# A two-layer transformer kernel on one core: prologue laid out anew, rows of maxima issued by ScalarE, last chunk worked by pairs of token tiles

## The reference

```
x0 = x0 + g_msa * mha(mod(ln(x0)))          # and x1 alike
x  = x + g_mca * cross(x0 <-> x1);  x = x + g_mlp * mlp(mod(ln(x)))
x  = ln(x + mha(x, mask)) ; x = ln(x + mha(x, ctx)) ; x = ln(x + mlp(x))
```

## Time and profile before

| what | value |
|---|---|
| median of 3 runs | 2251.17 us (2240.67 to 2251.61) |
| the profiled execution's own time | 2249.42 us |
| its span, first to last instruction | 2247.5 us |
| TensorE busy | 2020.5 us, 90% |
| VectorE, ScalarE, GpSimd busy | 1547.9, 1287.5, 552.3 us |
| maxima products L1415 | 2048, 526.3 us |
| score products L1394 and value products L1441 | 4224 each, 612.9 and 584.1 us |
| exponentials L1608 | 2112, 1100.8 us |

### The profile page before, as it was taken

The page is one execution under the profiler, slowest core; times in us unless marked ns, Lnnn a source line. Parts: engine busy times, 40 slices in busy tenths (PEclk is TensorE's granted clock), DMA queues, the critical chain, the costliest instruction groups (busy, mean ns, idle before and its releaser), DMA issues. The chain is left out here.

```text
span 2247.5 us, 33863 instructions
## 1 busy us (share of the span) xinstructions
PE 2020.5 (90%) x12890; PEld 794.0 (35%) x12890; DVE 1547.9 (69%) x2835; ACT 1287.5 (57%) x2406; POOL 552.3 (25%) x526
## 2 busy tenths in 40 slices
PE   4699899897979999998999888999999999999975
PEld 2423233332323343533533532332253335335324
DVE  4577689796967759476377457896757985895703
ACT  1035577565745677765675643678235874784650
POOL 0027586642132301032121332210103011101100
PEclk9769999998989999999999996999699999999987
DMA  6615243322052302035034431200120020000000
GB/s 150 135 57 127 74 133 84 102 58 48 17 136 61 76 5 54 20 69 121 8 75 96 76 77 55 58 20 21 34 47 28 4 49 4 13 16 4 13 16 11
DMA packets 97304, 126.65 MB, mean 56 GB/s; under 512 B 25293, under 2 KB 81982, under 8 KB 92014
## 3 DMA queue, kind: packets, MB, share of 16 engines
q1 hardware_dynamic: 97134, 124.42, 23.3%
HBM read 89.95 MB, written 24.74 MB: 51 GB/s over the span
## 5 line engine op out<-in xcount | busy, mean ns | idle before, releaser
L1608 ACT ACTIVATE PT<-ps 128x512 f32<-128x512 f32 (+1 forms) x2112 | 1100.8, 602 | 697.0 <-PE ps L1394 691.1
L1677 DVE TENSOR_REDUCE mx<-ps 128x1 f32<-128x512 f32 x2048 | 1283.3, 682 | 270.9 <-PE ps L1415 267.1
L1415 PE MATMUL ps<-KS,QS 49*128 49x512 bf16 x2048 | 526.3, 403 | 132.0 <-DVE mx L1677 78.7
L1394 PE MATMUL ps<-QS,KS 51*128 51x512 bf16 (+3 forms) x4224 | 612.9, 389 | 0.3
L1441 PE MATMUL ps<-PT,Vt 128*32 128x512 f32 (+1 forms) x4224 | 584.1, 626 | 0.0
L1415 PEld LDWEIGHTS ps<-KS,QS 49*128 49x128 bf16 x2048 | 146.2, 95 | 726.6 <-DVE mx L1677 479.8
L1394 PEld LDWEIGHTS ps<-QS,KS 51*128 51x128 bf16 (+3 forms) x4224 | 209.9, 97 | 255.3 <-ACT PT L1608 86.0
L1908 POOL CAST nm<-nm 128x16 bf16<-128x16 f32 x64 | 12.6, 197 | 524.4 <-DVE nm L1690 524.2
L1441 PEld LDWEIGHTS ps<-PT,Vt 128*32 128x32 f32 (+1 forms) x4224 | 84.3, 109 | 147.2 <-issue 144.6
L1536 PE MATMUL ps<-XT,big 128*128 128x256 f32 x512 | 125.7, 396 | 2.4 <-ACT big L1650 1.4
L1547 PE MATMUL ps<-big 128*128 128x256 f32 x512 | 114.7, 382 | 2.1 <-DVE big L1810 2.1
(11 more groups left out here) (104 smaller groups left out, 1076.8 us busy)
## 6 DMA issues: line engine op xcount, KB each, us to landing
scr<-S SPq DMA_DIRECT2D x28, 768.0 KB, 3.6
big<-in_mask_1x1xSxS_ik SPq DMA_DIRECT2D x16, 1024.0 KB, 4.8
QS<-scr SPq DMA_DIRECT2D x32, 384.0 KB, 8.5
KS<-scr SPq DMA_DIRECT2D x24, 384.0 KB, 8.4
QS<-scr SPq DMA_DIRECT2D x32, 256.0 KB, 4.9
ON<-Oe SPq DMA_DIRECT2D x256, 32.0 KB
OD<-scr_r SPq DMA_DIRECT2D x32, 256.0 KB
KS<-scr SPq DMA_DIRECT2D x24, 256.0 KB, 4.5
```

What stands on the lines that cost most here:

```text
L1394: z = eng.matmul(ps[0:w, it.bank[j], :], KS[lo:hi, part, pr, col:col + w], QS[lo:hi, part, u.qs, pr, :], start=part == 0, stop=part == 1 a ...
L1415: return eng.matmul(mbank(it)[:, 0:w], QS[lo:lo + MR, 0, u.qs, pr, 128 * it.tq:128 * it.tq + 128], KS[lo:lo + MR, 0, pr, it.lo:it.hi], sta ...
L1608: eng.activation(PT[0:w, it.pt * 4 + 2 * it.pp + j, :], ps[0:w, it.bank[j], :], ACT.Exp, scale=0.25).then_inc(S["exp_done"], 1)
L1677: eng.tensor_reduce(out=mx[:, u.b, c, it.i:it.i + 1], in_=mbank(it)[:, 0:it.hi - it.lo], axis=AX.X, op=ALU.max).then_inc(S["max_done"], 1)
```

## The change

Prologue: the memset of the V tile goes from the plan to VectorE's head. The head of SyncE loads only the bias columns it needs at once (`colb0_in`), then the constant rows, `bb` and `vb`; the other seven columns, chunks 2 and 3 of `x` and the two later parts of `ada_w` come as one item `late_load` after the transfers of K and Q. `mod_g` of modulation 0 is put behind Q of chunk 0; the first Q gets buffers of its own (`Qf[2]` = OD, `S3s[2]` in `big`) and a semaphore `scr_q`. Rows are read back in two parts: part 0 of K0, Q0, K1 first, then part 1 of all. Q of chunk 1 is now made by the ordinary way (GpSimd splits it). Modulations 1 and 2 and the gate bias leave `beside` and become the first five entries of `side`.

Maxima: the two transfers `QS<-mr` become an item of their own, `m_move`, one step later, on ScalarE.

Denominators: `dd<-Oe` is issued ahead of the four `ON<-Oe`, with a semaphore `d_out` for which VectorE's reciprocal waits. ScalarE's copy to `Oe` waits for `d_out` too.

Last chunk: `last_l1` in place of the general chain.

```diff
@@ do_qk, split
+                    quick_rows.append((lambda: to_dram(it), lambda part: to_rows(it, (part,))))
@@ fin_b
+                of, it = it, Item("m_move")
+                it.u, it.last, it.mr = u, of.last, of.mr
                 it.qs_free = mark.get(("qs_free", u.qs))
                 dma(it, "m_in", 2)
+                fins.append([FIN - 1, lambda: plan.append(it)])
@@ norm, nc_
+                for lo, hi in ((0, 256), (256, CH)) if at["tail"] else ((0, CH),):
+                    it = item("norm_c")
@@
+        def last_l1(c):
+            at["tail"] = True
+            flush_norms()
+            do_out(c, None, (1, 1), (0,))
+            do_stats(c, 1e-5, 1, 0, 2)
+            do_out(c, None, (1, 1), (2,))
+            do_lnscale(c, 1, 1, 0, 2)
+            do_stats(c, 1e-5, 1, 2, 2)
+            do_xt("x", c, cols=256)
+            do_hid(c, True, 24, 0, 0)
+            do_lnscale(c, 1, 1, 2, 2)
+            for hp in range(1, 4):
+                do_hid(c, True, 24, 0, hp)
+            do_xt("x", c, cols=256, t0=2)
+            do_mout(c, 0, 2, None, (0, 0))
+            do_hid(c, True, 24, 1, 0)
+            do_stats(c, 1e-5, 0, 0, 2)
+            for hp in range(1, 4):
+                do_hid(c, True, 24, 1, hp)
+            do_lnscale(c, 2, 0, 0, 2)
+            store(c, 0, 2)
+            for t in (2, 3):
+                do_mout(c, t, 1, None, (0, 0))
+            for t in (2, 3):
+                do_stats(c, 1e-5, 0, t, 1)
+                do_lnscale(c, 2, 0, t, 1)
+                store(c, t, 1)
+            at["tail"] = False
@@ prologue
         do_stats(0, 1e-6)
-        modulation(0)
         do_xnorm(0)
-        item("ones_v")
+        modulation("mod_t", 0)
         do_stats(1, 1e-6)
         do_xt("mod", 0, 0)
         do_xnorm(1)
-        drain(k_steps(0, 512, "k_in0", [], 0, 0, True))
-        drain(q_steps(0, 0, 0, 0, True))
+        drain(k_steps(0, 512, "k_in0", [], 0, 0, 1))
+        drain(q_steps(0, 0, 0, 0, 2))
+        (k0_out, k0_rows), (q0_out, q0_rows) = quick_rows
+        k0_out()
+        q0_out()
+        k0_rows(0)
+        q0_rows(0)
         do_xt("mod", 1, 0, 512, 1)
-        drain(k_steps(512, 512, "k_in1", [], 0, 1, True))
+        modulation("mod_g", 0)
+        drain(k_steps(512, 512, "k_in1", [], 0, 1, 1))
+        k1_out, k1_rows = quick_rows[2]
+        k1_out()
+        k1_rows(0)
+        for rows in (k0_rows, q0_rows, k1_rows):
+            rows(1)
+        item("late_load")
@@ beside
-        beside = [second_v, second_q, lambda: modulation(1), lambda: modulation(2),
-                  lambda: gate_bias(0, I["L0_xattn_attn_proj_b"])]
+        beside = [second_q, second_v, first_v]
@@
+        side.extend([lambda kind=kind, g=g: modulation(kind, g) for g in (1, 2) for kind in ("mod_t", "mod_g")])
+        side.append(lambda: gate_bias(0, I["L0_xattn_attn_proj_b"]))
-... early=[lambda: None, first_v])
+... early=[lambda: None, lambda: None])
@@ SyncE, evict_out
+                    load(eng, dd[32 * hg:32 * hg + 32, ob, :], Oe[16:128:32, 0, :], "d_out")
                     for j in range(4):
                         load(eng, ON[lo:lo + 16, hg // 2, :], Oe[32 * j:32 * j + 16, 0, :], "o_out")
-                    load(eng, dd[32 * hg:32 * hg + 32, ob, :], Oe[16:128:32, 0, :], "o_out")
@@ ScalarE
+                elif it.kind == "m_move":
+                    q.wait_ge(S["mr_done"], it.mr)
+                    q.wait_ge(S["m_in"], it.was)
+                    q.wait_ge(S["m_ready"], it.last)
+                    if it.qs_free is not None:
+                        q.wait_ge(S[it.qs_free[0]], it.qs_free[1])
+                    for t in range(2):
+                        load(eng, QS[49 + t:50 + t + 64:64, 0, u.qs, 2 * u.hg:2 * u.hg + 2, :], mr[16 * t:16 * t + 16, u.b, :], "m_in")
```

More of the change, by code:

```diff
@@ L254, in half @@
                 it.w = n["wq_in"] if q else n["wkv_in"]
-                it.qf_free = mark.get("qf_free") if quick else mark["xn_free"]
+                it.qf_free = mark.get(("qf_free", quick)) if quick else mark["xn_free"]
                 take_m(it)
@@ L272, in split @@
                     flush_ends()
-                later.extend([[SPLIT[0], flush_ends], [SPLIT[1], lambda: to_dram(it)]])
-                if quick:
-                    flush_later()
+                    quick_rows.append((lambda: to_dram(it), lambda part: to_rows(it, (part,))))
+                else:
+                    later.extend([[SPLIT[0], flush_ends], [SPLIT[1], lambda: to_dram(it)]])
             def split_end(of):
@@ L283, in to_dram @@
                 it = item("split_out")
-                it.cols, it.low = cols, of.low
+                it.cols, it.low, it.quick = cols, of.low, quick
                 of.k = it.k = 4 + slot if q else n["scr_use"] % 4
@@ L294, in to_dram, with to_rows @@
                     held_rows[slot] = lambda: to_rows(of)
-            def to_rows(of):
+            def to_rows(of, parts=(0, 1)):
                 it = item("split_in")
                 it.q, it.cols, it.lo, it.slot, it.k, it.out = q, cols, lo, slot, of.k, of.out
+                it.scr_sem, it.parts = of.scr_sem, parts
                 it.over = [mark[k] for k in [("qs_free", slot)] if k in mark] if q else over
                 it.lo_was, it.lo_sem = n[name.replace("in", "lo")], name.replace("in", "lo")
[L301 to L307, removed]
+                if 1 in parts:
+                    mark["scr_free", it.k] = (it.lo_sem, up(it.lo_sem, 32))
+                    if not q:
+                        mark["klo", name] = mark["scr_free", it.k]
+                if 0 in parts:
+                    dma(it, name, 4)
+                    if q:
+                        taken[slot] = True
+                    else:
+                        mark["k", name] = (name, it.landed)
             def second():
@@ L521, in do_out @@
             x_done, xn_free = n[f"x_done{c}"], mark["xn_free"]
-            for lo in (0, 2):
+            for lo in tiles:
                 it = item("out")
-                it.ot, it.w = n["ot_done"], n["wp_in"]
+                it.ot, it.w = n["ot_done"] - (1 if at["tail"] and lo == 0 else 0), n["wp_in"]
                 take_m(it)
@@ L900, in mlp0, with store @@
             return ln_mod(c, 2) + mlp_chain(c, False, 16, 2, (0, c // 2))
-        def mlp1(c):
[L903 to L920, removed]
+        def store(c, lo=0, nt=4):
+            it = item("store")
+            it.c, it.lo, it.nt = c, lo, nt
+            x_state(it, c)
+            dma(it, "y_out", 1)
@@ L921, in modulation @@
+        def modulation(kind, g):
+            it = item(kind)
+            it.g = g
+            it.ada = 16
+            take_m(it)
+            if kind == "mod_t":
+                it.t, it.done = up("mod_t"), up("mod_done")
+                give_m(it, ("mod_t", it.t))
+                return
+            give_m(it, ("mod_g", up("mod_g")))
             if g == 0:
@@ L1105, in fast @@
             bg_until(999)
-            at["tail"] = False
         def load_mask(c):
@@ L1266, in sp_part @@
                     for part, lo, t, k in ((0, 0, 0 if it.q else 2, 1), (0, 16, 0 if it.q else 1, 2), (1, 0, 0, 3)):
+                        if part not in it.parts:
+                            continue
                         if part == 1:
@@ L1380, in sp_part @@
                     q.wait_ge(S["y_out"], it.was)
-                    load(eng, chunk(out, it.c), x[:, 4 * it.c:4 * it.c + 4, :], "y_out")
+                    lo = 4 * it.c + it.lo
+                    load(eng, chunk(out, it.c)[:, it.lo:it.lo + it.nt, :], x[:, lo:lo + it.nt, :], "y_out")
         def pe_part(eng, q, items):
```

198 lines of the change are left out of this document (116 added, 82 removed), and 2 rows, old and new, of the table S.

## The result

The changed kernel takes 2235.37 us (median of 4 runs, 2233.78 to 2237.55), the kernel before 2251.39 in the same series (4 runs). The ratio is 0.993, 95% interval [0.9911, 0.995]: 16 us faster, where 33 were forecast. The profiled execution took 2233.78 us, span 2231.9.

| stretch | before | after | difference | forecast |
|---|---|---|---|---|
| start to first scores | 118.6 | 82.7 | -36.0 | -38.6 |
| first scores to the end of unit 0 | 48.6 | 63.2 | +14.7 | +11 |
| end of unit 0 to last copy of `Oe` (the middle) | 2003.6 | 2018.9 | +15.3 | +6 |
| last copy of `Oe` to the end | 76.7 | 67.1 | -9.6 | -10.8 |

What follows compares the result with a forecast made beforehand. TensorE was taken to bound the 2053 us middle, between a 118.6 us prologue and a 76 us tail. 2249.4 - 27.6 (net prologue) + 6 (maxima) - 10.8 (tail) = 2217, stated as 2218; range 2199 to 2238.

Steps and rivals of the forecast that it cites:

- Prologue: Start to first scores: a shorter chain of K, Q and first maxima, scores at 80, 38.6 us earlier.
- my 34: Prologue, from first maxima at 46 to first scores at 80: 34 us for unit 0's 32 maxima.
- What comes back: Unit 0: the modulations moved beside it, where TensorE is full, cost 11 us again.
- my upper bound of 13.6: Unit 0: the most the moved modulations could cost there, 13.6 us of TensorE; the lower bound was 0.
- Maxima issued by ScalarE: Middle: `QS<-mr` in ScalarE's queue delays exponentials in eight units by 0.75 us each, +6 us.
- Tail: After the last output copy: earlier denominators, last chunk by pairs, shorter end and smaller last store, -10.8 us.
- The 0.6 us for the product with OD in halves: Tail: the product with OD in halves lets the output projection start 0.6 us sooner.
- (a): Slower rival, middle: ScalarE's issues stall the exponentials in most units, +33 us, 2282; chance 0.05.
- My sign for it, above 40 us: Middle: TensorE's idle for exponentials above 40 us would show the rival of stalled exponentials.
- (b): Rival, prologue: transfers hold up Q's rows and low parts, scores start near 95, 2232; chance 0.17.
- (c): Rival, unit 0: the higher clock comes sooner, some 10 us more gained and modulations 3 cheaper, 2205; chance 0.15.
- the rule of the Trainium skill: Middle: an issue on ScalarE meeting one of SyncE's waits for a lock, holding exponentials longer; counted under the slow rival.

Runs made afterwards that it cites:

- mods_beside: first_act with modulations 1 and 2 and the gate bias back in the prologue, among unit 0's maxima; 2224.8 us, ratio 0.9883.
- first_act: The changed kernel with SyncE issuing `QS<-mr` without the extra step, except the first unit's, which ScalarE issues at once; 2215.8 us, ratio 0.9841.
- act_hold: The changed kernel with SyncE's Q rows, K rows and mask loads held until the last planned `QS<-mr` has landed; 2225.6 us, ratio 0.9881.
- m_sp: The changed kernel with all `QS<-mr` issued by SyncE again, without the extra step; 2222.8 us, ratio 0.9889.
- m_act_early: The changed kernel with `QS<-mr` still issued by ScalarE but without the extra step; 2240.8 us, ratio 0.9957.
- m_only: The kernel before with only this part of the change: `QS<-mr` issued by ScalarE, one step later; 2264.1 us, ratio 1.0059.
- m_sp_late: The changed kernel with `QS<-mr` issued by SyncE, but still one step later; 2238.0 us, ratio 0.9938.
- early_hold: m_act_early with SyncE's Q rows, K rows and mask loads held until the last planned `QS<-mr` has landed; 2224.4 us, ratio 0.9873.

## Why the prediction was right or wrong

**Prologue.** Right in each step: K products 16.7 for 17, K out 27.4 for 28, Q out 32.5 for 33, first maxima 45.3 for 46. The first scores came at 82.7 for 80: the 32 maxima took 3.4 us more than my 34, which I didn't test. The modulations were worth more there than the 13.6 us of the earlier trace rows: 20.5 by mods_beside, of which 3.7 were a wait for their weights.

**What comes back.** I took 11 us; it was 14.7 in unit 0, and the modulations' 15.75 us of TensorE, above even my upper bound of 13.6, account for it: without them beside it, unit 0 of mods_beside is as long as before. That bound was itself from rows in part at the higher level (2.84 us for a `mod_t`), while unit 0 ran at 0.50, where one takes 5.28. The bound at the level of the place where the work goes would have been right.

**Maxima issued by ScalarE: the step that failed.** I took +6 us, from eight exponentials' queues that would be held up. The middle grew by 15.3, and going back to SyncE gives 12.6 in the total even though this loses 12.8 in the prologue; with the prologue kept, in first_act, it gives 19.6. The place was wrong, too. An issue takes ScalarE 0.52 us beside running exponentials, and what showed was the wait for `QS<-mr` itself. What I overlooked is in two sentences of my own. "That SyncE stood 347.7 us waiting for `mr` made nobody else late": that wait, in order, was what kept the 1 MB and 384 KB transfers behind the 4 KB ones. And "the extra step of `fins` delays other transfers by a step that nobody waits for": GpSimd's product with OD is such a one, and TensorE waited for it 3.6 us at 1040.67. One thing in that paragraph held: one step later `mr` is ready and ScalarE's waits cost next to nothing (1.0 us, where it is 48.9 without the step).

Of the 19.6 us, act_hold shows 9.8 to be the order of transfers. The other 9.8 lie between act_hold and first_act, and what they are made of is not settled: the waits for GpSimd's product, which come with the step, are a part, and busy time of TensorE at the lower level another (busy in the middle 1875.4 us in the changed kernel, 1862.1 in m_sp, 1869.7 before), which differs between executions. Nor had I a term for what the rest of the change does to the middle: m_sp's is 12.3 us shorter than before in the profiled executions. That hid most of the cost in the changed kernel's 15.3, and no run tells where it comes from.

**Tail.** Right within 1.2 us: denominators 1.5 us earlier at `scr_r` (1.8 forecast), 5.7 from projection to MLP (6.5), 2.3 behind the last products (1.9). The 0.6 us for the product with OD in halves didn't come: from the issue of `scr_r<-dd` to the projection it is 7.7 us, 7.6 before. So the MLP starts 23.1 us after the last copy of `Oe` and not 21.

**The rivals.** (a) did not happen: TensorE's weight loads for score products waited for exponentials 87.3 us in the whole run, against 86.0 before. (My sign for it, above 40 us, could not have told: the kernel before is above it.) (b) came near in number (2232) and not in mechanism, since the first scores never came near 95. (c), the higher clock sooner: granted 0.67 by 100 to 120 us and 0.88 by 120 to 145, so the level rose earlier in the run. But it rose to stay only after 126 (0.50 in 116 to 126 us, 1.00 in 126 to 146), 43 us after the first scores, with one spell at the higher level ahead of that; before, it rose at 146 (0.50 in 142 to 146, 0.97 in 146 to 150), 27 us after them. So unit 0 had no less time at the lower level, and got no shorter. The sign was right. The size was half, for 9 us in the middle, 4 in unit 0, 3 ahead of the first scores and 1 in the tail.

**Two issuers at once.** At 354.82 the trace has two engines issuing, ScalarE 0.52 us in the middle of SyncE's 4.18 for six (3.19 before, 3.80 in m_sp), with an exponential running on ScalarE meanwhile. Of ScalarE's 128 issues in the changed kernel 27 meet one of SyncE's; they took 0.52 us as the median, like the other 101. On SyncE's side two of the six took 1.05 and 1.19 us and not 0.42, but in m_sp, with no second issuer, one took 1.55. So if a lock was waited for, it can't be seen on ScalarE. That speaks against the weight that I gave to the rule of the Trainium skill (Perfetto Trace Analysis, "DMA Instruction — HWDGE") by which the issuing sequencer first waits for an exclusive lock.

## What to carry to other kernels

A queue that stands waiting for its data is also an order: before a small, urgent transfer is taken out of the queue in which bulk stands behind it, ask what then goes out ahead of it. Where another engine must issue it, because the queue is full of other work (here the first unit alone), do so there and nowhere else, or hold the bulk back; and place the issue where its data is ready, or the engine stands still in its own queue. Price moved work at the clock of the place to which it goes.

## What the runs showed of the hardware

- A transfer of 4 KB issued by ScalarE 2 us behind SyncE's 1 MB, and among its 1.5 MB of Q rows, had its last packet after 13.6 us (changed kernel, 355.37). Behind the same 1 MB, but with the Q rows held back, it landed within 4.7 us (act_hold, issued at 347.54). The median of the changed kernel's 128 was 1.3. Issued by SyncE ahead of the same rows of Q, it made no one wait (m_sp).
- An issue on ScalarE took 0.52 to 0.56 us with an exponential running at the same time; the first two took 1.67 us together. Whether SyncE was issuing too made no difference to the median (0.52 us, 27 and 101 issues of the changed kernel).
- Standing in its queue for data that isn't ready does hold ScalarE's work up: 48.9 us in 46 times in m_act_early, 1.0 in 3 in the changed kernel, where the same issue stands one step later.
- Over the middle the 256 KB transfers `QS<-scr` landed after 6.0 us as the median in all three kernels measured with ScalarE as issuer without a hold (changed, m_act_early, m_only), and after 4.9 in before, m_sp, m_sp_late and first_act; with the hold 4.8 (act_hold, early_hold).
- A hole of 5.8 us in TensorE's work (changed kernel, 363.9 to 369.7) was followed by the lower clock, 0.59 in 372 to 376 us. The unit took 33.5 us, and 24.8 in act_hold and m_sp, which have no such hole.
- One kernel's executions differ by more than most single effects here: 22 us between the ends in the kernel before (27 runs), 23 in m_act_early (12), 18 in m_only (12), 16 in m_sp_late (10), 11 in m_sp (6), 5.6 in first_act (5). The numbers of runs differ, so these don't rank the kernels.
